# A chain of four attention and feed-forward layers on one core: sums a step sooner, casts in thirds, norms in halves, loads and weight work moved ahead, and an attention with turned keys

## The chip, the cores and the metric

One of the eight cores of a Trainium2 chip runs the whole program in one launch. The metric is the device time of one execution in microseconds (us); smaller is better. The times before are those of three runs; the profile is of one execution more.

## The reference, cut to what matters

x is 16 batches of 56 tokens of 128 features; the context is 16 batches of 1500 rows of 128. Each of four layers adds a cross-attention over the context and then a feed-forward, each on the layer norm of x:

```python
x = x + xattn_i(_layernorm(x), ctx, ...);  x = x + ffn_i(_layernorm(x), ...)   # i = 0, 1, 2, 3
# layers 0 and 3: 16 heads of 8; projections of queries, keys, values, softmax over 1500 keys, output
#   (layer 0 with biases and a mask)
# layer 1: 2 heads of 64; layernorm of the context and once more of x; keys and values are projected
#   from the context and from x (1556 in all); q and k are divided by their rms; masked softmax
# layer 2: 16 heads of 64; layernorm (eps 1e-6) of context, x and output; a null key and value beside
#   the 1500; sim = (xn Wq * scale) (cn Wk)^T; softmax; (attn cn Wv) Wo
# feed-forwards: 0: 8-bit tokens and ternary weights, gelu; 1 and 2: 8 experts, the two best gates
#   (hidden 512 and 256, relu); 3: ternary weights, gelu, layernorm
```

All of it is float32 but the scores of layers 0 and 3, where each factor is split into bfloat16 parts.

## The kernel before, in words

Tokens are held feature-first in xT (128 x 896); a tile is 112 tokens (two batches), 8 tiles in all. `build` runs eight stages in turn: L0a, L0f, L1a, L1f, L2a, L2f, L3a, L3f (attention and feed-forward of each layer). Each stage has a program for each of the five engines (a block), allocates its own tiles and semaphores, and begins with a barrier; `semaphores` clears its semaphores and puts one barrier more at its end. In a stage the order of the work on each engine is written out by hand; engines wait for counts of semaphores. So a stage's first load is issued after the stage before has ended on every engine.

**The norm** (`ln_pe`, `ln_dve`, `ln_pool`, `ln_turn`, lines 97 to 158). TensorE turns the eight token tiles (L100), VectorE takes statistics and adds eps (L133 to L138), GpSimd raises the eight variances to -0.5 (L122), VectorE normalises (L143), TensorE turns the tiles back (L112), VectorE copies (L155, L157). Each step takes all eight tiles before the next begins. In layers 1 and 2, whose attentions take a norm of the norm, the middle part runs twice (eps of two values).

**Attention of small heads** (`attention_16_small_heads`, layers 0 and 3). Eight heads of a batch's 16 make a stack, so there are 32 stacks (two a batch) with four groups of heads each. A step n is one group of one stack, 128 in all, eight a batch (t = n mod 8). In a step TensorE does scores of group n+6 for the maxima (L469 and L477; VectorE reduces them, L780 and L785), turned scores of group n with the maximum subtracted (units S, L504; ScalarE takes the exponential, L647), and the product of probabilities and values of the stack before (L491, part t mod 4 of its chunks). `SmallHeadUnits.of_step` (lines 272 to 290) adds other units to chosen steps: K and V (projections for a later batch, L508, L512), M (the row maxima of a stack, L517, after row_maxima, L792 to L796), R (the sums of the exponentials spread over the rows, L521; VectorE takes the reciprocal and multiplies, L769, L770) and Y (output projection). All units share a ring of four PSUM banks: a unit waits until the fourth before it is emptied, by VectorE (R, Y) or ScalarE (the others). R comes at t=1 and t=5. Stacks' sums are copied by ScalarE (L695) at t=3 and 7, and the values of the next stack wait for that copy. ScalarE also turns the mask to bfloat16 (`float_mask`, L678, t=1, layer 0 only) and the keys to their high bfloat16 part (`key_high`, L689, t=6 in layer 0, t=4 in layer 3), 128 x 1500 each. GpSimd makes the middle and low parts (L596 to L604), and SyncE's queue copies the parts, row by row, to the stacks (L420, L425, L429).

**Attention of layer 1** (`latent_attention`). SyncE loads raw rows and turned rows of a batch two ahead. Per batch: statistics of the raw rows (`stats`, L1218 on), powers on GpSimd, projections K and V, squares and `key_sums`, GpSimd's `key_norm` (L1106, L1110), transposes of the keys (T2), scores, `maximum` (L1268), exponential (L1195), transposes (T3), product (O), transpose (Z), output (Y). Before the loop K and V of batches 0 and 1 are both made, then the first scores.

**Attention of layer 2** (`attention_16_wide_heads`). Wq Wk^T of each head (L1554) and Wv Wo (L1572) are folded to 128 x 128, after VectorE has worked the context norm's scale and bias into Wk and Wv (`weights`, L1742 to L1751). Each batch has 896 rows (16 heads x 56), seven tiles of 128; a step is one tile: three scores matmuls of 501 keys for tile n+2 (L1515), `maximum` on VectorE (L1731), exponential on ScalarE (L1655), 12 transposes of the probabilities in units T0, T1, T2 (L1529), the product with the values in unit O (L1534) of tile n-1, scaled by the reciprocal of the sum by ScalarE (L1646). VectorE normalises the raw rows of the next batch (`normalise`, L1721, t=1 to 3) into V; the keys are V's transposes (unit K, three a batch, L1542, copied by L1707). Unit Z (two a batch, L1546) turns the seven products back. K and Z are `extra(n)` of `WideHeadUnits`. GpSimd raises all variances of the context to -0.5 at the stage's start (L1627) and is idle in the loop. After the loop the output projection runs over all heads (L1608), then a norm and the addition to x.

## Time and profile before

| what | value |
|---|---|
| median of three runs | 2398.16 us (2397.18 to 2400.27) |
| the profiled execution | 2396.25 us, its span 2394.5 us |
| TensorE busy | 2147.7 us (90%), mean granted clock 0.935 |
| VectorE, ScalarE, GpSimd busy | 1443.5, 1203.0, 608.6 us |
| layer 0: attention, feed-forward (TensorE's first and last instruction) | 6 to 455, 456 to 520 |
| layer 1 | 522 to 825, 827 to 946 |
| layer 2 | 949 to 1826, 1830 to 1902 |
| layer 3 | 1905 to 2343, 2344 to 2390 |

```profile
PE   6999999637999698799999999999996889999995
DVE  5677677568888344645544555455434567776775
PEclk8999999757999899799999999999997989999996
```

Each digit is a fortieth of the span, 59.9 us, in tenths of busy time; PEclk is TensorE's granted clock in tenths of 2.4 GHz. The clock falls at the starts of stages, where TensorE is least busy.

### The profile page before, as it was taken

Reading aid. Unit: us, or ns where it says so; the run is one execution under the profiler, and the core shown is the slowest. Engines: PE = TensorE matmul, PEld = TensorE weight load, DVE = VectorE, ACT = ScalarE, POOL = GpSimd, SP = SyncE. Lnnn points to the kernel's source line nnn. Section 1 sums busy time; section 2 is a strip of 40 time slices with the busy share of each in tenths; the row PEclk is TensorE's granted clock in tenths of the full one; section 3 lists DMA queues with packets and bytes.
Section 4 is the critical chain, followed back from the end, with each engine's and each line's share of the span. In section 5 each row is a group of like instructions: output and inputs, shape, how many; then the busy total and the mean of one; then the engine's idle time right before and its main releaser. Section 6 shows DMA issues by size and latency. Waiting matters only on the chain. (4 is left out here: it accounts for less than half of the span.)

```text
span 2394.5 us, 48823 instructions
## 1 busy us (share of the span) xinstructions
PE 2147.7 (90%) x19446; PEld 1583.1 (66%) x19446; DVE 1443.5 (60%) x3160; ACT 1203.0 (50%) x2251; POOL 608.6 (25%) x233
## 2 busy tenths in 40 slices
PE   6999999637999698799999999999996889999995
PEld 3666666426888554467777777777773456766773
DVE  5677677568888344645544555455434567776775
ACT  5777776304666332244444444444430366767761
POOL 7656554004666200600000000000000063433400
PEclk8999999757999899799999999999997989999996
DMA  6444444012442001200000000000000254444420
GB/s 167 139 143 130 137 128 114 14 51 82 132 124 77 19 27 51 59 17 17 20 31 17 17 23 27 17 17 17 1 1 14 64 155 124 122 139 130 115 62 17
DMA packets 87072, 165.19 MB, mean 69 GB/s; under 512 B 40384, under 2 KB 48624, under 8 KB 86592
## 3 DMA queue, kind: packets, MB, share of 16 engines
q1 hardware_dynamic: 86848, 162.08, 23.5%
q8 instruction: 156, 2.56, 0.5%
q14 instruction: 68, 0.56, 0.1%
HBM read 81.75 MB, written 0.46 MB: 34 GB/s over the span
## 5 line engine op out<-in xcount | busy, mean ns | idle before, releaser
L1534 PEld LDWEIGHTS L2ps<-L2values,L2probsT 125*128 125x128 f32 (+1 forms) x2688 | 317.5, 192 | 50.6 <-issue 49.6
L1515 PE MATMUL L2ps<-L2keys,L2qz 128*128 128x501 f32 x672 | 340.1, 590 | 0.9 <-DVE L2out_bias L1778 0.9
L1534 PE MATMUL L2ps<-L2values,L2probsT 125*128 125x128 f32 (+1 forms) x2688 | 318.4, 275 | 0.0
L1731 DVE CUSTOM_DVE_ANT_0 L2work<-L2ps,L2maskadd,L2big 128x1503 f32<-128x1503 f32 x112 | 199.8, 1783 | 163.2 <-PE L2ps L1515 163.2
L122 POOL TENSOR_TENSOR rstd<-mv,half_neg 112x8 f32<-112x8 f32 x9 | 16.8, 1866 | 983.3 <-DVE mv L138 983.3
L1529 PEld LDWEIGHTS L2ps<-const,L2work 128*126 128x126 f32 x1344 | 163.8, 140 | 116.3 <-issue 64.7
L647 ACT ACTIVATE L3probsT<-L3ps 128x448 f32<-128x448 f32 x384 | 191.8, 547 | 84.9 <-PE L3ps L504 84.7
L647 ACT ACTIVATE L0probsT<-L0ps 128x448 f32<-128x448 f32 x384 | 193.0, 550 | 66.1 <-PE L0ps L504 66.0
L1529 PE MATMUL L2ps<-const,L2work 128*126 128x128 f32 x1344 | 202.2, 273 | 1.6 <-ACT L2work L1655 0.9
L785 DVE TENSOR_REDUCE L0partmax<-L0ps 112x1 f32<-112x1000 f32 x128 | 153.3, 1197 | 72.1 <-PE L0ps L477 71.9
L1646 ACT ACTIVATE L2z<-L2ps,L2rinv 128x128 f32<-128x128 f32 x112 | 41.1, 367 | 304.8 <-PE L2ps L1534 304.8
L785 DVE TENSOR_REDUCE L3partmax<-L3ps 112x1 f32<-112x1000 f32 x128 | 153.2, 1197 | 64.1 <-PE L3ps L477 63.8
L1655 ACT ACTIVATE L2work<-L2work,L2negmax 128x1503 f32<-128x1503 f32 x112 | 172.4, 1540 | 15.9 <-DVE L2negmax L1731 15.9
L1639 ACT COPY L2probsT<-L2ps 126x512 f32<-126x512 f32 x224 | 129.5, 578 | 100.3 <-PE L2ps L1529 100.2
L1702 DVE COPY L2probsT<-L2ps 126x512 f32<-126x512 f32 x112 | 77.4, 691 | 147.1 <-PE L2ps L1529 147.1
L504 PEld LDWEIGHTS L3ps<-L3query_stack,L3key_stack 98*128 98x128 bf16 x1536 | 110.6, 99 | 59.2 <-issue 16.3
L504 PEld LDWEIGHTS L0ps<-L0query_stack,L0key_stack 99*128 99x128 bf16 x1536 | 110.4, 99 | 59.6 <-issue 15.5
L504 PE MATMUL L3ps<-L3query_stack,L3key_stack 98*128 98x112 bf16 x1536 | 135.5, 214 | 0.8 <-DVE L3heads_out L770 0.4
L504 PE MATMUL L0ps<-L0query_stack,L0key_stack 99*128 99x112 bf16 x1536 | 135.2, 213 | 0.7 <-ACT L0probsT L647 0.2
L780 DVE TENSOR_REDUCE L0partmax<-L0ps 112x1 f32<-112x500 f32 x128 | 86.4, 675 | 40.0 <-PE L0ps L469 38.3
L780 DVE TENSOR_REDUCE L3partmax<-L3ps 112x1 f32<-112x500 f32 x128 | 86.4, 675 | 38.8 <-PE L3ps L469 37.1
L491 PE MATMUL L0ps<-L0probsT,L0values 128*32 128x112 f32 x3072 | 99.7, 263 | 7.6 <-ACT L0osum L695 7.6
(463 smaller groups left out, 4180.3 us busy)
## 6 DMA issues: line engine op xcount, KB each, us to landing
L0key_stack<-L0key_parts SPq DMA_DIRECT2D x192, 187.5 KB
L3key_stack<-L3key_parts SPq DMA_DIRECT2D x192, 187.5 KB
L0ctxT<-in_ctxT SPq DMA_DIRECT2D x16, 750.0 KB, 4.5
L1raw<-in_ctx SPq DMA_DIRECT2D x16, 750.0 KB
L1rawT<-in_ctxT SPq DMA_DIRECT2D x16, 750.0 KB, 6.2
L2raw<-in_ctx SPq DMA_DIRECT2D x16, 750.0 KB
L3ctxT<-in_ctxT SPq DMA_DIRECT2D x16, 750.0 KB, 4.5
L1fw<-in_L_w SPq DMA_DIRECT2D x16, 256.0 KB, 2.9
```

Of the source, the lines that this page charges most:

```text
L491: last = nc.tensor.matmul(PS[32 * g:32 * g + 32, 3, u * TT:(u + 1) * TT], V[:, b % 2, value_columns(c, 4 * u + g)], PT[:, u, c, g, :], sta ...
L504: last = nc.tensor.matmul(PS[:, bank, c * TT:(c + 1) * TT], KS[:, h % 4, tau, key_columns(4 * j + c)], QS[:, h % 4, tau, :], start=True, s ...
L647: ins = nc.scalar.activation(PT[:, h % 2, 4 * j:4 * j + 4, tau, :], PS[:, bank, 0:HALF].rearrange("p (c n) -> p c n", c=4), ACT.Exp)
L780: nc.vector.tensor_reduce(PM[:, h % 2, tau, 0:1], PS[0:TT, 0, 0:500], AX.X, ALU.max).then_inc(s.m0_done, 1)
L785: nc.vector.tensor_reduce(PM[:, h % 2, tau, 1:2], PS[0:TT, 1:3, 0:500], AX.XY, ALU.max).then_inc(s.m12_done, 1)
L1515: last = nc.tensor.matmul(PS[:, 3 * (m % 2) + c, 0:NPR], tile_rows(m), KT[:, m // RT % 2, 500 * c:500 * c + NPR], start=True, stop=True)
L1529: last = nc.tensor.transpose(PS[0:CH + 1, bank, c * P:(c + 1) * P], PR[:, i % 2, at:at + CH + 1], k.ident)
L1534: last = nc.tensor.matmul(PS[:, bank, 0:P], PT[0:keys_in(c), i % 2, c, :], V[0:keys_in(c), i // RT % 2, c, :], start=c == 0, stop=c == NCH ...
L1639: ins = nc.scalar.copy(PT[:, i % 2, 4 * j:4 * j + 4, :].rearrange("p c n -> p (c n)"), PS[0:CH + 1, bank, :])
L1655: nc.scalar.activation(PR[:, m % 2, :], SM[:, m % 2, :], ACT.Exp, bias=nmax[:, m % 4:m % 4 + 1], scale=-1.0, accum_out=ssum[:, m % 4:m % 4 ...
L1702: ins = nc.vector.tensor_copy(PT[:, i % 2, 4 * j:4 * j + 4, :].rearrange("p c n -> p (c n)"), PS[0:CH + 1, bank, :])
L1731: nc.vector.tensor_tensor_reduce(SM[:, m % 2, :].rearrange("p (c n) -> p c n", c=3), PS[:, 3 * (m % 2):3 * (m % 2) + 3, 0:NPR], MA[:, m // ...
```

## The change

The norm works in halves of four tiles, and the norm of a norm becomes one pass: its variance v gives v (1 + eps2) + eps1 eps2, and one power is taken.

```diff
+    for h in range(2):
+        pe.wait_ge(s.ln_norm, h + 1)
+        for t in range(4):
+            last = nc.tensor.transpose(ps[:, 2 + h, t * TT:(t + 1) * TT], k.xn[:, 4 * h + t, :], k.ident[0:TT, 0:TT])
+        last.then_inc(s.ln_feat, 1)
...
+def ln_pool(pool, k, s):
     nc = k.nc
-    for n in range(len(eps)):
-        pool.wait_ge(s.ln_var, n + 1)
-        nc.gpsimd.tensor_tensor(k.rstd[:], k.mv[:, :, 1], k.half_neg[0:TT, 0:NTT],
+    for h in range(2):
+        pool.wait_ge(s.ln_var, h + 1)
+        nc.gpsimd.tensor_tensor(k.rstd[:, 4 * h:4 * h + 4], k.mv[:, 4 * h:4 * h + 4, 1], k.half_neg[0:TT, 0:4],
                                 ALU.pow).then_inc(s.ln_rstd, 1)
...
+    for h in range(2):
+        tiles = range(4 * h, 4 * h + 4)
+        dve.wait_ge(s.ln_tok, h + 1)
+        for t in tiles:
             last = nc.vector.bn_stats(k.stats[:, t, :], src(t))
         link(last)
...
+        var = k.mv[:, 4 * h:4 * h + 4, 1]
+        if len(eps) == 1:
+            last = nc.vector.tensor_scalar(var, var, eps[0], None, ALU.add)
+        else:
+            last = nc.vector.tensor_scalar(var, var, 1.0 + eps[1], eps[0] * eps[1], ALU.mult, ALU.add)
+        last.then_inc(s.ln_var, 1)
...
+    for h in range(2):
+        dve.wait_ge(s.ln_rstd, h + 1)
+        for t in range(4 * h, 4 * h + 4):
...
-    last.then_inc(s.ln_norm, 1)
+        last.then_inc(s.ln_norm, 1)
```

In the small heads R moves to t=0 and t=4, and the two casts are made in thirds of 500 columns, at t=0, 1, 2 (mask) and t=6, 7, 8 (high part in layer 0) or 3, 4, 5 (layer 3).

```diff
-        if t == 1 and 0 <= 2 * b - 2 < HB:
+        if t == 0 and 0 <= 2 * b - 2 < HB:
             own.append(("R", 2 * b - 2, 0, "D"))
-        if t == 5 and 0 <= 2 * b - 1 < HB:
+        if t == 4 and 0 <= 2 * b - 1 < HB:
             own.append(("R", 2 * b - 1, 0, "D"))
...
-                nc.scalar.copy(KP[:, b % 2, 0], KF[:, b % 2, :]).then_inc(s.hi_ready, 1)
+            def float_mask(b, thirds=range(3)):
+                for j in thirds:
+                    if j == 0:
+                        wait_mask(act, b)
+                        if b:
+                            act.wait_ge(s.keys_masked, b)
+                    at = slice(j * 500, (j + 1) * 500)
+                    nc.scalar.copy(MF[:, at], MR[:, b % 2, at]).then_inc(s.mask_float, 1)
...
+            def key_high(b, thirds=range(3)):
+
+                for j in thirds:
+                    if masked:
+                        act.wait_ge(s.keys_masked, b + 1)
+                    else:
+                        wait_emptied(act, plan.emptied("K", b, j))
+                    if b >= 2 and j == 0:
+                        wait_stacked(act, 2 * b - 4)
+                        wait_stacked(act, 2 * b - 3)
+                    at = slice(j * 500, (j + 1) * 500)
+                    nc.scalar.copy(KP[:, b % 2, 0, at], KF[:, b % 2, at]).then_inc(s.hi_ready, 1)
...
-                if masked and n % 8 == 1 and 3 <= n // 8 + 3 < B:
-                    float_mask(n // 8 + 3)
-                if n % 8 == (6 if masked else 4) and 3 <= n // 8 + 3 < B:
-                    key_high(n // 8 + 3)
+                if masked and n % 8 in (0, 1, 2) and 3 <= n // 8 + 3 < B:
+                    float_mask(n // 8 + 3, [n % 8])
+                b, j = divmod(n - (6 if masked else 3), 8)
+                if j < 3 and 3 <= b + 3 < B:
+                    key_high(b + 3, [j])
```

`LatentAhead` owns the tiles of layer 1's loads, and its seven first loads are issued in the feed-forward of layer 0 (`ahead.sync(sp)`, behind that stage's own). In layer 1 batch 1's K and V, its squares and its statistics are placed behind the first scores.

```diff
+    def sync(self, sp):
+        sp.dma_start(self.W[:], self.src["L1_attn_w"]).then_inc(self.s.w_loaded, 16)
+        for b in range(2):
+            self.load_raw(sp, b)
+            self.load_turned(sp, b)
+            self.load_mask(sp, b)
...
-    units = kv(0, (0, 1)) + kv(0, (2,)) + kv(1, (0, 1)) + kv(1, (2,)) + turned_keys(0)
+    units = kv(0, (0, 1, 2)) + turned_keys(0) + kv(1, (0, 1, 2))
...
-            for what, j in (("K", 0), ("V", 0), ("K", 1), ("V", 1)):
-                unit(what, 0, j)
...
-            unit("K", 0, 2)
-            unit("V", 0, 2)
+            for j in range(3):
+                unit("K", 0, j)
+                unit("V", 0, j)
...
-            for what, j in (("K", 0), ("V", 0), ("K", 1), ("V", 1)):
-                unit(what, 1, j)
...
-            unit("K", 1, 2)
-            unit("V", 1, 2)
             for j in range(3):
                 unit("T2", 0, j)
             scores(0, range(4))
+            for j in range(3):
+                unit("K", 1, j)
+                unit("V", 1, j)
...
+            stats(0)
+            dve.wait_ge(s.qk_filled, 1)
...
-            last.then_inc(s.vl_ready, 1)
+            key_sums(0)
+            stats(1)
...
-            empty("K", 1, 2)
             empty("T2", 0, 1)
+            maximum(0)
+            for j in range(3):
+                empty("K", 1, j)
             stats(2)
             key_sums(1)
```

`WideAhead` does the same for layer 2's weights in layer 1's feed-forward: loads, the work of `weights` on GpSimd, with the sums on VectorE before the experts 5 and 6 (`vector`), and the powers of the context's variances.

```diff
+    def sync(self, sp):
+        s = self.s
+        for n in (1, 2, 0, 3):
+            sp.dma_start(self.W[:, n], self.src["L2_attn_w"][:, n]).then_inc(s.w_loaded, 16)
...
+        pool.wait_ge(s.w_loaded, 64)
...
+        for n in (1, 2):
+            w = self.W[:, n]
+            nc.gpsimd.tensor_tensor(self.products[:, n - 1], w, self.ROWS[:, 1:2, :].to_broadcast([64, 16, P]), ALU.mult
+                                    ).then_inc(s.products, 1)
+            pool.wait_ge(s.products, n)
+            nc.gpsimd.tensor_tensor(w, w, self.ROWS[:, 0:1, :].to_broadcast([64, 16, P]), ALU.mult).then_inc(s.scaled, 1)
+            pool.wait_ge(s.scaled, n)
+            nc.gpsimd.tensor_tensor(w[:, :, 0:P - 1], w[:, :, 0:P - 1], w[:, :, P - 1:P].to_broadcast([64, 16, P - 1]),
+                                    ALU.subtract).then_inc(s.centred, 1)
+        pool.wait_ge(s.ve_ready, 1)
+        for pair in range(B // 2):
+            at = self.rs[:, 2 * pair:2 * pair + 2, :].rearrange("p b c -> p (b c)")
+            nc.gpsimd.tensor_tensor(at, at, self.k.half_neg[0:CH, 0:24], ALU.pow).then_inc(s.spread, 1)
...
+    def vector(self, dve, link, n):
+
+        nc, s = self.nc, self.s
+        dve.wait_ge(s.products, n)
+        link(nc.vector.tensor_reduce(self.U[:, n - 1], self.products[:, n - 1], AX.X, ALU.add))
+        dve.wait_ge(s.centred, n)
+        dve.wait_ge(s.rows_loaded, 48)
+        nc.vector.tensor_scalar(self.W[:, n, :, P - 1], self.U[:, n - 1], -1.0, self.NKV[:, n - 1:n], ALU.mult, ALU.add
+                                ).then_inc(s.summed, 1)
```

In layer 2 the units K (but for batch 0) and Z are gone. The turned rows of the context are loaded into the key tile, and GpSimd subtracts the mean and multiplies by the reciprocal deviation; both are written once to DRAM and loaded per batch, spread over 127 partitions. O's operands are exchanged, so that its product comes out turned, and the division by the sum is made on the probabilities before their transposes (`scale`, on VectorE).

```diff
+        SCALE_OF = WQK[:].rearrange("p h n -> p (h n)")[0:P - 1, 0:S2]
...
+            def load_keys(b):
+                if b == 1:
+                    sp.wait_ge(s.slot_ready, 2)
+                    sp.wait_ge(s.q_filled, 2 * H)
+                else:
+                    sp.wait_ge(s.scores_filled, RT * (b - 1))
+                    sp.wait_ge(s.keys_scaled, b - 1)
+                sp.dma_start(KT[0:P - 1, b % 2, 0:S2], src["ctxT"][b][0:P - 1]).then_inc(s.key_parts, 16)
+                for x, to in enumerate((MEAN[0:P - 1], SCALE_OF)):
+                    sp.dma_start(to, scratch[x, b].rearrange("c n -> (c n)").partition_broadcast(P - 1)).then_inc(s.key_parts, 16)
...
+            sp.wait_ge(s.moments_ready, 1)
+            sp.dma_start(scratch.rearrange("k (h b) c n -> (b c) (k h) n", h=2), MOMENTS[:]).then_inc(s.moments_stored, 16)
+            sp.wait_ge(s.moments_stored, 16)
+            load_keys(1)
...
+                    if m == 0:
                         for j in range(3):
-                            wait_emptied(pe, plan.emptied("K", m // RT, j))
+                            wait_emptied(pe, plan.emptied("K", 0, j))
+                    elif m % RT == 0:
+                        pe.wait_ge(s.keys_scaled, m // RT)
...
-                        pe.wait_ge(s.exp_done, i + 1)
+                        pe.wait_ge(s.scaled, i + 1)
...
-                        last = nc.tensor.matmul(PS[:, bank, 0:P], PT[0:keys_in(c), i % 2, c, :], V[0:keys_in(c), i // RT % 2, c, :],
+                        last = nc.tensor.matmul(PS[:, bank, 0:P], V[0:keys_in(c), i // RT % 2, c, :], PT[0:keys_in(c), i % 2, c, :],
...
-                elif what == "Z":
-                    wait_emptied(pe, plan.emptied("O", RT * i + (6 if j else 3), 0))
-                    for t in range(3 if j else 4):
-                        last = nc.tensor.transpose(PS[:, bank, t * P:(t + 1) * P], ZB[:, j, t, :], k.ident)
...
+            for n in range(4):
+                half_of = slice(n % 2 * (B // 2), n % 2 * (B // 2) + B // 2)
+                of = rs[:, half_of, :] if n >= 2 else k.ctx_mv[:, half_of, :, 0]
+                last = nc.tensor.transpose(PS[0:B // 2 * NCH, 5, n * CH:(n + 1) * CH], of.rearrange("p b c -> p (b c)"),
+                                           k.ident[0:CH, 0:CH])
...
-            for pair in range(B // 2):
...
+            nc.gpsimd.memset(KT[:, 1, :], 0.0).then_inc(s.slot_ready, 1)
+            pool.wait_ge(s.slot_ready, 1)
+            nc.gpsimd.tensor_copy(KT[:, 1, S2:S2 + 1], k.ident[:, P - 1:P]).then_inc(s.slot_ready, 1)
+            for b in range(1, B):
+                pool.wait_ge(s.key_parts, 48 * b)
+                nc.gpsimd.tensor_tensor(KT[0:P - 1, b % 2, 0:S2], KT[0:P - 1, b % 2, 0:S2], MEAN[0:P - 1], ALU.subtract
+                                        ).then_inc(s.keys_moved, 1)
+                pool.wait_ge(s.keys_moved, b)
+                nc.gpsimd.tensor_tensor(KT[0:P - 1, b % 2, 0:S2], KT[0:P - 1, b % 2, 0:S2], SCALE_OF, ALU.mult
+                                        ).then_inc(s.keys_scaled, 1)
...
-                    g = t // 4
-                    if b:
-                        act.wait_ge(s.filled, plan.filled("Z", b - 1, g))
-                    act.wait_ge(s.rinv_ready, i + 1)
-                    ins = nc.scalar.mul(ZB[:, g, t % 4, :], PS[:, bank, 0:P], rinv[:, i % 4:i % 4 + 1])
+                    ins = nc.scalar.copy(tile_rows(i), PS[:, bank, 0:P])
...
-                    if i >= 2:
-                        dve.wait_ge(s.scores_filled, RT * (i - 1))
                     ins = nc.vector.tensor_copy(KT[:, i % 2, 500 * j:500 * j + n], PS[:, bank, 0:n])
-                elif what == "Z":
-                    n = (3 if j else 4) * P
-                    ins = nc.vector.tensor_copy(QZ[:, i, 4 * P * j:4 * P * j + n], PS[:, bank, 0:n])
...
+            def scale(m):
+
+                dve.wait_ge(s.exp_done, m + 1)
+                nc.vector.reciprocal(rinv[:, m % 4:m % 4 + 1], ssum[:, m % 4:m % 4 + 1]).then_inc(s.rinv_ready, 1)
+                dve.wait_ge(s.rinv_ready, m + 1)
+                nc.vector.tensor_scalar(PR[:, m % 2, :], PR[:, m % 2, :], rinv[:, m % 4:m % 4 + 1], None, ALU.mult
+                                        ).then_inc(s.scaled, 1)
...
+            scale(0)
             for n in range(plan.last_step + 1):
                 b, t = divmod(n, RT)
                 if plan.first(n):
                     empty(*plan.first(n))
-                if n < RT * B:
-                    dve.wait_ge(s.exp_done, n + 1)
-                    if n >= 4:
-                        dve.wait_ge(s.emptied_a, plan.emptied("O", n - 4, 0)[1])
-                    nc.vector.reciprocal(rinv[:, n % 4:n % 4 + 1], ssum[:, n % 4:n % 4 + 1]).then_inc(s.rinv_ready, 1)
-                if plan.extra(n):
-                    empty(*plan.extra(n))
                 if t in (1, 2, 3) and b + 1 < B:
                     normalise(b + 1, t - 1)
+                if n + 1 < RT * B:
+                    scale(n + 1)
                 if n + 2 < RT * B:
                     maximum(n + 2)
```

## Rows read from the trace of the kernel before

**Rows 1.** Stretches: each engine's busy time (instructions), granted clock, DMA share, GB/s.

```profile
60.00:440.00 380.00, 360.10 (x5379) 261.34 (x5381) 268.78 (x458) 276.22 (x541) 192.78 (x67) 1.00 0.44 125
...
522.00:586.00 64.00, 38.14 (x223) 33.19 (x223) 47.41 (x181) 15.73 (x32) 24.94 (x12) 0.66 0.33 103
...
949.00:1023.00 74.00, 51.42 (x191) 33.40 (x192) 44.00 (x95) 14.82 (x25) 41.51 (x14) 0.71 0.29 69
...
1040.00:1790.00 750.00, 748.61 (x4932) 587.05 (x4930) 372.03 (x688) 346.07 (x565) 0.00 (x0) 1.00 0.06 18
```

**Rows 2.** Timeline, layer 0: start, us, engine, line, operation, tiles, [idle <-releaser].

```profile
234.10 0.38 PE L469 MATMUL L0ps<-L0key_stack,L0query_stack 97*112 97x500 bf16 x1
...
235.67 0.85 DVE L769 RECIPROCAL L0ps<-L0ps 128x112 f32<-128x112 f32 x1
...
236.88 0.36 PE L517 MATMUL L0ps<-L0ident_bf,L0maxparts 112*3 112x112 bf16 x4 [0.74 <-DVE L0heads_out L770]
...
238.31 0.38 PE L469 MATMUL L0ps<-L0key_stack,L0query_stack 97*112 97x500 bf16 x1
...
248.43 0.38 PE L469 MATMUL L0ps<-L0key_stack,L0query_stack 97*112 97x500 bf16 x1
...
252.10 0.38 PE L469 MATMUL L0ps<-L0key_stack,L0query_stack 97*112 97x500 bf16 x1
...
254.18 0.38 PE L469 MATMUL L0ps<-L0key_stack,L0query_stack 97*112 97x500 bf16 x1
...
255.34 0.78 PE L491 MATMUL L0ps<-L0probsT,L0values 128*32 128x112 f32 x24 [0.59 <-ACT L0osum L695]
...
257.81 0.38 PE L469 MATMUL L0ps<-L0key_stack,L0query_stack 97*112 97x500 bf16 x1
```

**Rows 3.** Timeline, layer 3: the same wait.

```profile
2103.06 0.36 PE L517 MATMUL L3ps<-L3ident_bf,L3maxparts 112*2 112x112 bf16 x4 [0.74 <-DVE L3heads_out L770]
```

**Rows 4.** Timeline, layer 2's loop: a step with K, one with neither.

```profile
1286.09 0.60 PE L1529 MATMUL L2ps<-const,L2work 128*126 128x128 f32 x4
...
1287.81 0.59 PE L1542 MATMUL L2ps<-const,L2values 125*128 125x125 f32 x4
1288.24 1.01 PE L1515 MATMUL L2ps<-L2keys,L2qz 128*128 128x501 f32 x2
...
1293.04 0.60 PE L1529 MATMUL L2ps<-const,L2work 128*126 128x128 f32 x4
...
1306.95 0.60 PE L1529 MATMUL L2ps<-const,L2work 128*126 128x128 f32 x4
...
1307.42 1.54 ACT L1655 ACTIVATE L2work<-L2work,L2negmax 128x1503 f32<-128x1503 f32 x1
...
1310.99 1.78 DVE L1731 CUSTOM_DVE_ANT_0 L2work<-L2ps,L2maskadd,L2big 128x1503 f32<-128x1503 f32 x1 [2.64 <-PE L2ps L1515]
...
1313.47 0.60 PE L1529 MATMUL L2ps<-const,L2work 128*126 128x128 f32 x4
```

**Rows 5.** Layer 1's and 3's starts, and a group (busy, mean ns | idle).

```profile
552.49 0.69 DVE L1291 TENSOR_SCALAR L1keysT<-xnT,vec 128x896 f32<-128x896 f32 x1
...
1905.39 1.32 DVE L801 TENSOR_SCALAR L3head_scale<-const 128x2 f32<-128x2 f32 x1 [1.14 <-PEq L78]
...
L598 POOL TENSOR_TENSOR L3keys<-L3keys,L3key_parts 128x1500 f32<-128x1500 f32 x16 | 48.6, 3035 | 200.5 <-ACT L3key_parts L689 200.5
```

**Rows 6.** Timeline, layer 1's start (the stage begins at 522.1).

```profile
534.22 2.42 DVE L1218 BATCH_NORM_STATS2 L1st<-L1raw 125x6 f32<-125x128 f32 x12 [6.97 <-DMA L1raw<-in_ctx]
...
586.13 1.78 DVE L1268 CUSTOM_DVE_ANT_0 L1masked<-L1ps,L1maskadd 112x1556 f32<-112x1556 f32 x1 [1.16 <-PE L1ps L1031]
```

**Rows 7.** Timeline, layer 2's start (the stage begins at 949.0).

```profile
980.54 20.93 PE L1566 MATMUL L2ps<-xnT,L2wqk 128*128 128x448 f32 x46 [1.49 <-DVE xnT L157]
...
1020.73 8.25 PE L1515 MATMUL L2ps<-L2keys,L2qz 128*128 128x501 f32 x12 [0.87 <-DVE L2out_bias L1778]
```

**Rows 8.** Timeline, layer 1's feed-forward, its norm.

```profile
832.64 2.64 DVE L143 TENSOR_SCALAR xn<-L1fps,mv,rstd 112x128 f32<-112x128 f32 x8 [1.76 <-POOL rstd L122]
...
837.13 1.16 DVE L155 COPY xnT<-L1fps 128x448 f32<-128x448 f32 x2 [1.85 <-PE L1fps L112]
```

357 lines of the change are left out of this document (159 added, 198 removed).

## The prediction

> **What bounds it now.** I read the stretches first [rows 1]: in the small-head loop of layer 0 TensorE is busy 360 of 380 us, in the wide-head loop of layer 2 748.6 of 750. There the time is TensorE's own list plus its stalls. In the two stretches between loops (522 to 586, 949 to 1023) it is busy only 38 and 51 us, at a granted clock of 0.66 and 0.71; there the longest chain through VectorE, GpSimd and the loads counts. Then the timelines. A step of the small-head loop is the distance between two L469 matmuls. The eight steps of a batch repeat to 0.01 us in twelve batches: 4.21, 2.98, 3.87, 3.26, 3.67, 2.08, 3.63, 2.35, sum 26.05; [rows 2] show four of them. The step without additions lasts 2.08 (252.10 to 254.18). In layer 2 a batch is 47.70: steps of 6.95 where a unit K or Z is added, 6.52 where none is [rows 4], all gapless. The change is therefore priced per step in the loops and along a chain in the prologues.
>
> **Small heads, sums sooner.** M (L517) starts at 236.88 after 0.74 idle, released by L770, which follows the reciprocal at 235.67, which stands behind row_maxima in VectorE's order [rows 2]. Without the stall the step of 4.21 is 2.08 + 0.28 (M) + 0.90 (K, 2.98 - 2.08) = 3.26: the stall is 0.95. The step of 3.67 has 2.08 + 0.28 + 0.89 (V): 0.41. The edit puts R a step earlier, in steps without row_maxima, so M waits for ScalarE units only. What is late next is row_maxima itself: R (1.13 us) in t=0 moves max0 of t=1 back to 2.03 after the step's start, so the maxima are ready 2.08 into t=2, where M wants to start at 1.9: 0.25 stays. In t=4 R is emptied 4.26 into a step of 4.14, and the first S of t=5 waits for it at 4.35: no stall, with 0.1 to spare. Gain 0.70 x 15 + 0.41 x 14 = 16.2. Layer 3 stalls the same way [rows 3]: 16.1 more. Bounds: 6 if the tight place in t=4 opens, 20 if no remainder stays.
>
> **Casts in thirds.** In layer 0 the whole cast on ScalarE delays the copy of the sums, and the values matmul waits 0.59 at 255.34; the step of 3.63 should be 2.97 (Y costs 0.89) [rows 2]. Three casts of about 0.6 for one of 1.45 add 0.7 us to a ScalarE that then has 21.4 of about 24.5 us filled; by adding up the steps it falls 0.8 us behind in t=6 to 2 (mask third and key third meet in t=0), and the copy of the sums comes 0.2 late. I take 0.45 x 12 = 5.4. Bounds: 7.9 and -6 (two units of the ring late per batch). The parts of the keys get ready 4 us later; their slot comes free only about then, and the stack lands 8 us before its first scores. The first stack is on the chain: +0.7. Layer 3's ScalarE has no mask to cast: 0. Layer 0 in all: -20.8 (with its share of 16.1).
>
> **Layer 2's loop.** Transposes K: 12 a batch, 0.43 for 4 (1287.81 to the next S) [rows 4]; Z: 7 a batch, 0.43 and 0.33. 3 x 0.43 + 0.76 = 2.05 a batch, and all steps become 6.52: 15 x 2.05 = 30.8, and 1.9 in the last batch with its emptying. The exchanged operands of O keep count and sizes: 0 (bounds +-0.02 a step). New on VectorE: scale(n+1), 1503 columns in place. A like instruction took 0.69 for 896 columns [rows 5], so about 1.0; bound above 1.6 (no faster than a cycle an element). Its place: exp ends 2.3 after the first transpose of a step (1307.42 + 1.7 - 1306.95), scale runs from 2.5 to 3.7, the maximum waits for its scores till 4.04 (1310.99) and ends at 5.9, exp needs it at 7.0 [rows 4]. With normalise (1.05 us) before it, scale ends at 4.0; both hide. TensorE waits for scale(n+1) only at the next step. Cover gone by over a microsecond, each microsecond more costs 112.
>
> GpSimd, idle until now in this loop, gets two operations of 3.04 a batch [rows 5]. Two numbers there say that the two engines keep each other out: L801, two elements wide, took 1.32, as long as GpSimd's memset that ran beside it. A scale held up by 3.0 pushes the exponential back by about 1.3 at worst. One scale in each batch can be met: 0 to 20 in all; I take 4. The Trainium skill ("SBUF — State Buffer", section "SBUF: two separate sides") says that the shared port pair is an exclusive lock, held for a whole instruction, for a VectorE instruction in a two-port mode against GpSimd. The trace agrees (the 1.32 us). The mechanism's own price, if both operations of a batch reached TensorE at full length, is rival (e).
>
> Keys: three loads of 762 KB a batch, 2.3 MB, then 6.1 us of GpSimd, from two steps before a batch to two steps before the next, 45.6 us. At the 69 GB/s that [rows 1] show at worst, 33 + 6.1: hidden. Loop: 32.7 - 4 = -28.7.
>
> **Layer 2's start.** Old: first scores 71.7 us after the stage's start (949.0 to 1020.73), projection of the queries from 980.54 [rows 7]. The weight work moves into layer 1's feed-forward: GpSimd there six operations of some 4.1 and eight of 4.5 (61 us; from the weights' landing near 845 it ends before 920, the stage at 946); VectorE two sums of 2.3 that fit its waits of 2.8 for TensorE. New chain: tokens 1.0, norm 5.9, folds meanwhile on TensorE to 9.5, turning and copies to 12.2, then 32 projections. Before, these ran 1.5 us each for the first 5 us and 0.75 after; I keep that (clock at 1.2 GHz after the sparse matmuls before them): 27.4 with normalise(0). Then 3.8 each for the folds of the values, the bias and the first keys: 51.0. Gain 20.7; less 2.3, since scale(0) stands behind maximum(1). -18.4; bounds -27 (2.4 GHz throughout) and -6 (1.2 GHz as long as before).
>
> **Layer 1's start.** VectorE waited 6.97 us for the raw rows, and the first maximum came 64 us in [rows 6]. All six loads now lie in layer 0's feed-forward, whose queue is empty; its own weights go first. One pass of the norm less is 4.8 us. Along the new order: norm 7.4, folds and turning 11.5, stats(0) 15.1, query copies and K(0) 20.4, squares and sums 27.6, powers and norm on GpSimd 35.6, queries turned 38.6, scores 45.2: the first maximum 18.7 sooner. But K and V of batch 1, stats(2) and key_sums(1) now come behind it, and GpSimd's norm of batch 1 ends at 64: the second maximum at 72 where it was at 83.3. -11.3; bounds -4 and -19.
>
> **Norms in halves.** The power on GpSimd (1.76 idle) and the turning (1.85 idle, then both copies) are overlapped with the other half [rows 8]: 1.5 net of the added instructions, 1.5 for the turning, 0.5 to 0.9 for tokens. Layer 0's feed-forward 1.5 (no turning; VectorE starts there with the weights' sums), layer 1's 3.3, layer 2's output 3.3, its feed-forward 3.7, layer 3's 3.0 (waits for weights). In layers 0 and 3 attention the keys' chain is longer: 0. Less 1.0, where GpSimd's weight work meets the gates: -13.8; bounds -8 and -16. Two more groups of semaphores to clear: +0.6 (1.38 between layer 2's stages, which clears two, against 1.15).
>
> **Sum** against the profiled execution, 2396.25 (span 2394.5; median of the runs 2398.16, 0.08% above): 20.8 + 16.1 + 28.7 + 18.4 + 11.3 + 13.8 - 0.6 = 108.5, so 2288.
>
> **Rivals.** (a) Prologues and thirds give little: the waits are handed to the next late chain (GpSimd's powers in layer 1, the 1.2 GHz clock in layer 2), the thirds cost as much as they give. What is left are the steps TensorE doesn't have to run: 16 + 14 + 27 + 6 + 4 + 8, less 5: about 2326. For it: TensorE had work from 970, and the projections from 980.54 still ran at 1.5 us each for 5 us. (b) TensorE stays at 2.4 GHz through both prologues, and nothing meets on the port: 2396 less 128 = 2268. Against it: both stretches still hold gaps of several microseconds. (c) Slower: the keys come late. One row sent to 127 partitions is no load that these rows show at this size. With everything else as forecast (80 us), the kernel gets slower once the chain of loads and two operations takes over 47.7 + 80 / 15 = 53 us; at 60 us it gives 2316 + 15 x 12.3 = 2500. Against it: 33 us at the worst rate. (d) The change doesn't do what it says in the small heads: S of t=5 waits for R as long as M did before, 2288 + 32 = 2320. For it: 0.1 us of margin. (e) GpSimd's two operations hold VectorE off for their whole 6.1 us, and TensorE waits: 2288 - 4 + 15 x 6.1 = 2375. For it: L801 [rows 5]; against it: a hold-up of 3.0 meets 1.7 us of slack between scale, maximum and exponential.
>
> **Chances.** Forecast 0.60, (a) 0.17, (b) 0.09, (c) 0.05, (d) 0.05, (e) 0.04. A change under 0.2% can't be told from none here; only a (c) of just 53 us gives that: 0.01 of its 0.05, so faster 0.95, slower 0.04; I shade this to 0.93, 0.02 and 0.05 for what six edits at once may do to each other. The range goes from (b) to just beyond (a): 2265 to 2332.
>
> **What would show it.** Layer 2: all steps 6.52, exp_done to scale short, GpSimd's key operations done long before the batch; wrong, if L1529's first transpose waits for the scaling. Small heads: batches of 24.0 to 24.6, no idle before L517 from L770; wrong, if S of t=5 waits for R. Layer 1: no load wait at the first statistics, first maximum near 45. Layer 2's first scores near 51. The forecast fails by more than its range only if a batch of layer 2 isn't about 45.6.

## The result: slower by 28%, because the keys of layer 2 come late

The changed kernel takes 3067.59 us (median; 3061.77 to 3077.04), the kernel before 2397.67. The ratio is 1.2796, interval 1.2761 to 1.2831. Forecast were 2288 and a range of 2265 to 2332: wrong in sign and size. What happened is rival (c), to which the prediction gave 0.05.

The page of the changed kernel, its 40 slices (76.7 us each):

```profile
PE   7999975899698456533664336643466388899996
POOL 6556602566340000000000000000000000544320
PEclk8999985999798778766887678866787688999997
GB/s 151 154 147 139 129 83 22 125 115 58 49 35 38 35 37 26 36 36 36 37 26 36 36 36 28 34 36 36 37 26 35 14 8 58 142 141 135 130 109 14
```

TensorE is half idle from the 14th to the 32nd slice, and the core moves mostly 26 to 38 GB/s there, against 130 to 150 in layers 0 and 3. The costliest group says who is waited for, and the stretch says how much (columns as in [rows 1] and [rows 5]):

```profile
L1596 PE MATMUL L2ps<-L2keys,L2qz 128*128 128x501 f32 x672 | 366.9, 631 | 731.5 <-POOL L2keys L1713 730.6
L1710 POOL TENSOR_TENSOR L2keys<-L2keys,L2mean_spread 127x1500 f32<-127x1500 f32 x15 | 50.1, 3339 | 1388.1 <-DMA L2wqk<-L_moments 1388.1
...
1040.00:2480.00 1440.00, 727.29 (x4456) 551.49 (x4457) 422.83 (x694) 326.95 (x544) 100.17 (x30) 0.75 0.09 32
```

The 730.6 us are 15 waits, one a batch: six steps of a batch last 6.52 us, the seventh (t=5, in which the first scores of the next batch stand) 54.1 to 59.4. Who makes GpSimd wait stands in the DMA queue of SyncE; a long row there is an issue that SyncE could not finish:

```profile
1260.91 0.23 SPq L1569 DMA_DIRECT2D L2keys<-in_ctxT  x1
1261.18 0.54 SPq L1571 DMA_DIRECT2D L2mean_spread<-L_moments  x1
1261.77 29.86 SPq L1571 DMA_DIRECT2D L2wqk<-L_moments  x1
1291.67 28.93 SPq L1552 DMA_DIRECT2D L2raw<-in_ctx  x1
1320.64 17.14 SPq L1557 DMA_DIRECT2D L2mask<-in_mask_full  x1
...
1350.56 3.34 POOL L1710 TENSOR_TENSOR L2keys<-L2keys,L2mean_spread 127x1500 f32<-127x1500 f32 x1 [89.72 <-DMA L2wqk<-L_moments]
1353.98 3.34 POOL L1713 TENSOR_TENSOR L2keys<-L2keys,L2wqk 127x1500 f32<-127x1500 f32 x1
...
1357.46 2.01 PE L1596 MATMUL L2ps<-L2keys,L2qz 128*128 128x501 f32 x2 [48.45 <-POOL L2keys L1713]
```

From the issue at 1260.91 to the landing at 1350.5 pass 89.6 us for three loads of 127 rows, 29.9 each. With GpSimd's 6.8 that makes 96.4, and the next loads are issued at 1357.39: loads and operations form one ring, because mean and deviation have one tile each. While only these loads run, packets of 6000 bytes end every 0.229 us, one after the other:

```profile
1265.00:1290.00 25.00, 25.00 (x163) 19.42 (x162) 14.18 (x22) 10.20 (x18) 0.00 (x0) 0.99 0.07 27
```

A DMA share of 0.07 is one sixteenth: one of the core's 16 DMA engines works. 127 packets x 0.229 = 29.1 us. After each idle stretch TensorE starts again at 1.2 GHz (granted clock 0.50 from 1357.4 to 1359.5; the first two scores above took 2.01 us, 1.01 in the running loop). The loop's excess over steps of 6.52 is 767 us, 730.6 of it waiting; the other 2.4 us a batch go with these slow restarts.

By stage, TensorE's first to last instruction, in us, one profiled execution of each kernel. The last column is the changed kernel with two repairs (below), in which nothing hides the other steps:

| stage | before | forecast change | changed kernel | with both repairs |
|---|---|---|---|---|
| layer 0 attention | 448.6 | -20.8 | 430.1 (-18.5) | 427.7 (-20.9) |
| its feed-forward | 63.2 | -1.5 | 62.0 (-1.2) | 62.0 (-1.2) |
| layer 1 attention | 303.4 | -11.3 | 292.3 (-11.1) | 291.8 (-11.6) |
| its feed-forward | 118.9 | -2.3 | 129.5 (+10.6) | 117.3 (-1.6) |
| layer 2 attention | 876.8 | -50.4 | 1588.6 (+711.8) | 816.9 (-59.9) |
| its feed-forward | 72.7 | -3.7 | 69.1 (-3.6) | 69.0 (-3.7) |
| layer 3 attention | 437.2 | -16.1 | 425.1 (-12.1) | 422.4 (-14.8) |
| its feed-forward | 45.8 | -3.0 | 42.9 (-2.9) | 43.0 (-2.8) |

Six of eight stages lie within 4 us of the forecast; layer 2's attention is off by 762. The second, small miss is layer 1's feed-forward, by 13. Its gates' chain on VectorE (rows of the timeline; GpSimd's operations below):

```profile
814.22 0.20 DVE L2251 CAST L1fgate_short<-L1fgate 112x64 bf16<-112x64 f32 x1
814.45 0.20 DVE L2252 CAST L1fgate_parts<-L1fgate_short 112x64 f32<-112x64 bf16 x1
814.56 4.52 DVE L2253 TENSOR_TENSOR L1fgate<-L1fgate,L1fgate_short 112x64 f32<-112x64 f32 x1
819.12 4.50 DVE L2254 CAST L1fgate_short<-L1fgate 112x64 bf16<-112x64 f32 x1
823.65 3.61 DVE L2255 CAST L1fgate_parts<-L1fgate_short 112x64 f32<-112x64 bf16 x1
827.18 0.21 DVE L2256 TENSOR_TENSOR L1fgate_parts<-L1fgate,L1fgate_short 112x64 f32<-112x64 f32 x1
...
814.50 4.50 POOL L1421 TENSOR_TENSOR L2qz<-L2work,L2lnc_rows 64x2048 f32<-64x2048 f32 x1 [13.17 <-DMA L2nkv<-in_L_null]
819.08 4.49 POOL L1424 TENSOR_TENSOR L2work<-L2work,L2lnc_rows 64x2048 f32<-64x2048 f32 x1
823.64 3.57 POOL L1426 TENSOR_TENSOR L2work<-L2work 64x2032 f32<-64x2032 f32 x1
```

Three instructions of 0.2 us last exactly as long as the GpSimd operation beside each. 12.0 us are lost, and TensorE waits 11.8 us for the gates' parts.

### The profile page after: what moved, and what is told of

Its sections match the earlier page's. It is cut to its first block and busy times, and to the rows that moved or that the text cites. A ratio compares the mean times of both kernels' runs of the same rounds, so it can differ in the third digit from the quotient of the medians.

```text
span 3067.4 us, 48086 instructions
## 1 busy us (share of the span) xinstructions
PE 2150.3 (70%) x19158; PEld 1575.0 (51%) x19158; DVE 1501.3 (49%) x3143; ACT 1208.0 (39%) x2353; POOL 730.9 (24%) x278
## 3 DMA queue, kind: packets, MB, share of 16 engines
q1 hardware_dynamic: 93008, 196.56, 20.9%
## 5 line engine op out<-in xcount | busy, mean ns | idle before, releaser
L1596 PE MATMUL L2ps<-L2keys,L2qz 128*128 128x501 f32 x672 | 366.9, 631 | 731.5 <-POOL L2keys L1713 730.6
L1596 PEld LDWEIGHTS L2ps<-L2keys,L2qz 128*128 128x128 f32 x672 | 110.8, 207 | 738.3 <-issue 737.1
L1710 POOL TENSOR_TENSOR L2keys<-L2keys,L2mean_spread 127x1500 f32<-127x1500 f32 x15 | 50.1, 3339 | 1388.1 <-DMA L2wqk<-L_moments 1388.1
L1615 PEld LDWEIGHTS L2ps<-L2probsT,L2values 125*128 125x128 f32 (+1 forms) x2688 | 317.5, 192 | 51.5 <-issue 49.9
L1615 PE MATMUL L2ps<-L2probsT,L2values 125*128 125x128 f32 (+1 forms) x2688 | 318.4, 275 | 0.5 <-ACT L2probsT L1725 0.5
L1610 PEld LDWEIGHTS L2ps<-const,L2work 128*126 128x126 f32 x1344 | 173.0, 146 | 135.0 <-issue 133.1
L1610 PE MATMUL L2ps<-const,L2work 128*126 128x128 f32 x1344 | 212.2, 282 | 3.5 <-DVE L2work L1817 3.1
L1727 ACT COPY L2qz<-L2ps 128x128 f32<-128x128 f32 x112 | 29.7, 265 | 305.7 <-PE L2ps L1615 305.7
L1817 DVE TENSOR_SCALAR L2work<-L2work,L2rinv 128x1503 f32<-128x1503 f32 x112 | 112.3, 1003 | 3.9
L791 DVE TENSOR_REDUCE L0partmax<-L0ps 112x1 f32<-112x500 f32 x128 | 86.2, 673 | 33.6 <-PE L0ps L474 33.5
```

Of the source, the lines that this page charges most:

```text
L791: nc.vector.tensor_reduce(PM[:, h % 2, tau, 0:1], PS[0:TT, 0, 0:500], AX.X, ALU.max).then_inc(s.m0_done, 1)
L1596: last = nc.tensor.matmul(PS[:, 3 * (m % 2) + c, 0:NPR], tile_rows(m), KT[:, m // RT % 2, 500 * c:500 * c + NPR], start=True, stop=True)
L1610: last = nc.tensor.transpose(PS[0:CH + 1, bank, c * P:(c + 1) * P], PR[:, i % 2, at:at + CH + 1], k.ident)
L1615: last = nc.tensor.matmul(PS[:, bank, 0:P], V[0:keys_in(c), i // RT % 2, c, :], PT[0:keys_in(c), i % 2, c, :], start=c == 0, stop=c == NCH ...
L1817: nc.vector.tensor_scalar(PR[:, m % 2, :], PR[:, m % 2, :], rinv[:, m % 4:m % 4 + 1], None, ALU.mult).then_inc(s.scaled, 1)
```

## Experiments

All stand beside runs of the kernel before on the same chip, but not all on one chip: the kernel before took 2397.3 us beside e1, e3, e4 and e5, 2399.3 beside e6 to e9 and 2402.0 (one run) beside e2 and e10. Between these groups a distance of medians is good to a few us only; there the ratios and the stages of the traces count. Stages whose code an edit leaves alone differ by up to 4 us between the profiled executions: in the nine kernels that have the changed kernel's code there, layer 0's attention took 427.7 to 431.2 us and layer 3's 422.4 to 426.3, most of it at the start of the loops.

First, what makes a load of 127 rows slow.

**e1_112**

```diff
-    sp.dma_start(KT[0:P - 1, b % 2, 0:S2], src["ctxT"][b][0:P - 1]).then_inc(s.key_parts, 16)
-    for x, to in enumerate((MEAN[0:P - 1], SCALE_OF)):
-        sp.dma_start(to, scratch[x, b].rearrange("c n -> (c n)").partition_broadcast(P - 1)).then_inc(s.key_parts, 16)
+    for lo, hi in ((0, 112), (112, 127)):
+        sp.dma_start(KT[lo:hi, b % 2, 0:S2], src["ctxT"][b][lo:hi]).then_inc(s.key_parts, 16)
+    for lo, hi in ((0, 112), (112, 127)):
+        for x, to in enumerate((MEAN[lo:hi], SCALE_OF[lo:hi])):
+            sp.dma_start(to, scratch[x, b].rearrange("c n -> (c n)").partition_broadcast(hi - lo)).then_inc(s.key_parts, 16)
```

> The changed kernel with one edit: each of the three key loads of a batch in layer 2 is cut into two DMAs, rows 0 to 111 and rows 112 to 126. Theory A (a load of 127 rows runs on one DMA engine, one 6000-byte packet each 0.229 us, so 29.1 us a load): 112 rows are 7 packets on each of 16 engines, 1.6 us, the loads leave the path, all batches of layer 2's loop last 45.6 us as the fourth steps now wait for nothing, and the time is 3067.6 less the waits above 6.52 us in the loop (767 us): 2300 us. Theory B (sending one row of DRAM to many partitions is slow by itself): two loads of three stay at 29 us, a batch takes 67 us, 2620. Theory C (GpSimd's two key operations, now beside a running loop, hold VectorE up for their whole length): 2300 + 15 x 6.7 = 2400.

Measured 2303.04, ratio 0.9611 (0.9594 to 0.9628). Theory A: the bytes are the same, and the loss is gone. A batch lasts 45.64 us throughout, but for one of 45.91. GpSimd's first operation starts 13.4 us after the issue instead of 89.6. Right behind the issues of a batch (1156.46 to 1159.1) all 16 DMA engines work (the last three numbers are the clock, the DMA share and GB/s):

```profile
1158.00:1164.00 6.00, 6.00 (x39) 4.52 (x39) 3.04 (x6) 2.89 (x5) 0.00 (x0) 1.00 1.00 292
```

Theory C falls too: the operations meet VectorE now, and the steps stay. Of 112 scales 18 overlap an operation and 14 are held by it. The timeline at the worst of them:

```profile
1259.17 4.17 DVE L1819 TENSOR_SCALAR L2work<-L2work,L2rinv 128x1503 f32<-128x1503 f32 x1
1259.19 3.35 POOL L1712 TENSOR_TENSOR L2keys<-L2keys,L2mean_spread 127x1500 f32<-127x1500 f32 x1 [36.88 <-DMA L2wqk<-L_moments]
...
1263.26 1.77 DVE L1810 CUSTOM_DVE_ANT_0 L2work<-L2ps,L2maskadd,L2big 128x1503 f32<-128x1503 f32 x1
```

The scale takes 4.17 us for 1.00; the step it is in takes 6.79 for 6.52. All the rest is slack.

**e2_keys** cuts only the load of the turned rows; its diff to e1_112 is

```diff
     for lo, hi in ((0, 112), (112, 127)):
         sp.dma_start(KT[lo:hi, b % 2, 0:S2], src["ctxT"][b][lo:hi]).then_inc(s.key_parts, 16)
-    for lo, hi in ((0, 112), (112, 127)):
+    for lo, hi in ((0, 127),):
         for x, to in enumerate((MEAN[lo:hi], SCALE_OF[lo:hi])):
```

and **e3_spreads**, the other way round, has `((0, 127),)` in the first of these loops and cuts only the two spreading loads.

> The changed kernel with only the load of the turned rows cut at row 112; the two spreading loads stay whole (127 rows). Theory A (every load of 127 rows takes 29.1 us on one engine, and the loads of a batch, GpSimd's 6.8 us and the next batch's loads form one chain): 58.2 + 3 + 2.2 + 6.8 = 70 us at most, 68 at least, for a batch, so 2303 + 15 x 23.5 = 2655. Theory B (the loads of a batch would run side by side on other engines if the first did not block them): 2303.

> The changed kernel with only the two loads that spread mean and deviation cut at row 112; the load of the turned rows stays whole (127 rows). Theory A (one engine for 127 rows): the chain of a batch is 29.1 + some 3 + 2.2 us until all has landed + 6.8 of GpSimd = 41 us, under the 45.6 of the loop, so the time is that of e1_112, 2300. Theory B (a load of 29 us also holds back the raw rows and the mask on the same queue): waits of a few us at every fourth step, 2300 to 2400.

Measured 2654.55 and 2309.29 (one run each, profiled). Each load left whole costs its 29 us of the ring, until the ring is shorter than the batch: the operations start every 70.1 to 71.1 us with two whole loads (72.5 the first time). That e2_keys meets the expected 2655 to the microsecond is in part luck: layer 2's attention is 366 us longer than in e1_112, not 352, and layer 1's feed-forward, which the edit leaves alone, is 16 us shorter (see e5_gates). With one whole load the ring is about as long as the batch, 45 to 47 us, longer than the 41 expected, since the last spreading load is issued only some 18 us behind the whole one; a step is late by up to 1.3 us in nine batches, and the first batch loses 3.8. So e3 lies 6 us above e1_112 (9 us in layer 2's attention), as its theory B has it in part: a slow load holds back what is issued behind it. The spreading as such is cheap. GpSimd's first operation in e2_keys:

```profile
1226.34 3.34 POOL L1712 TENSOR_TENSOR L2keys<-L2keys,L2mean_spread 127x1500 f32<-127x1500 f32 x1 [63.62 <-DMA L2wqk<-L_moments]
1296.56 3.34 POOL L1712 TENSOR_TENSOR L2keys<-L2keys,L2mean_spread 127x1500 f32<-127x1500 f32 x1 [63.45 <-DMA L2wqk<-L_moments]
```

**e4_113**: all three cut at row 113, a prime.

```diff
-    for lo, hi in ((0, 112), (112, 127)):
+    for lo, hi in ((0, 113), (113, 127)):
```

> The changed kernel with the three key loads cut at row 113 instead of 112 (rows 0 to 112, and 14 rows). Theory A (the number of engines is the largest number up to 16 that divides the rows; 113 is a prime): each big load still runs on one engine, 113 x 0.229 = 25.9 us, a batch takes 97 - 3 x 3.2 = 87 us, and the time is 2300 + 15 x 42 = 2930. Theory B (only the full length of 127 rows is badly placed, or the size of a DMA counts): like e1_112, 2300.

Measured 2930.19 (one run), where A said 2930; again the exact number is partly luck. The operations start every 88 to 90 us, not 87, and layer 2's attention is 639 us longer than in e1_112, while layer 1's feed-forward is 15 us shorter there. So one row more in the large part costs 639 us in its stage, and issues behind such a load stand for 25.4 to 26.1 us, with a DMA share of 0.07:

```profile
1228.46 25.51 SPq L1573 DMA_DIRECT2D L2wqk<-L_moments  x1
```

Neither the length nor the size of a DMA decides, but whether the number of rows can be divided over the engines.

**e10_gpsimd**: the whole loads of 127 rows again, issued by GpSimd (this one and all that follow have the repair of the gates, next).

```diff
+    pool.dma_start(KT[0:P - 1, b % 2, 0:S2], src["ctxT"][b][0:P - 1]).then_inc(s.key_parts, 16)
+    for x, to in enumerate((MEAN[0:P - 1], SCALE_OF)):
+        pool.dma_start(to, scratch[x, b].rearrange("c n -> (c n)").partition_broadcast(P - 1)).then_inc(s.key_parts, 16)
     pool.wait_ge(s.key_parts, 48 * b)
```

> The changed kernel with the gates' order of e5_gates, all three key loads whole (127 rows), but issued by GpSimd on its own queue, right before it waits for them. Theory A (the split over engines follows the same division of rows whoever issues): 29.1 us a load as before, 3067.6 less 21 = 3046. Theory B (GpSimd's queue spreads 127 rows over 16 engines, as the Trainium skill, DMA: Bandwidth & Descriptors, section Why a DMA increments its semaphore by 16 and not by 1, states for some direct copies): the chain of a batch is 3 x 2 + some 5 us for issuing and landing + 6.8 = 18 us, hidden, time 2282 to 2290. Theory C (the keys were late because the raw rows and the mask lay ahead of them on SyncE's queue): one engine, but no queueing, 87 + 6.8 = 94 us a batch, 3010.

Measured 2288.8 (one run), its theory B. In the timeline the three loads of 127 rows are issued in 1.6 us, and GpSimd's first operation starts 12.7 us after the first issue:

```profile
1233.09 0.57 POOL L1704 DMA_DIRECT2D L2keys<-in_ctxT  x1 [26.18 <-PE L2ps L1584]
1233.65 0.52 POOL L1706 DMA_DIRECT2D L2mean_spread<-L_moments  x1
1234.16 0.52 POOL L1706 DMA_DIRECT2D L2wqk<-L_moments  x1
1245.76 3.36 POOL L1708 TENSOR_TENSOR L2keys<-L2keys,L2mean_spread 127x1500 f32<-127x1500 f32 x1 [11.07 <-DMA L2wqk<-L_moments]
```

```profile
1235.00:1245.00 10.00, 10.00 (x64) 7.51 (x63) 5.24 (x8) 5.26 (x9) 0.00 (x0) 1.00 0.96 221
```

2.29 MB in 12.7 us are 180 GB/s where one engine gave 27, and the DMA share meanwhile is 0.96: all 16 engines. So of the two queues tried only SyncE's puts 127 rows on one engine. The Trainium skill ("DMA: Bandwidth & Descriptors", section "Why a DMA increments its semaphore by 16 and not by 1") states both: a DMA runs on the largest number of engines up to 16 that divides the slowest dimension (here the rows) of both its sides, with 127 as an example for one engine, and, as an exception on trn2, GpSimd's queue gives some direct copies all 16. The runs agree: 29 us behind each load of 127 rows and 26 behind one of 113 on SyncE's queue, and 12.7 us for three loads of 127 from GpSimd.

**e5_gates**: e1_112, and GpSimd waits for the gates' parts before the weight work.

```diff
             if ahead:
+                pool.wait_ge(s.parts_ready, 1)
                 ahead.gpsimd(pool)
```

> As e1_112, and in layer 1's feed-forward GpSimd begins layer 2's weight work only after VectorE has made the parts of the gates. Theory A (a copy on VectorE that meets a GpSimd operation waits for its end: three copies of 64 elements took 4.5, 4.5 and 3.6 us in the changed kernel): the gate chain loses some 11.5 us, the stage goes from 129.5 to 118, and the time is 11.5 below e1_112, about 2288.5. Theory B (the gates are late because the weights' loads share the queue or the memory): within 1 us of e1_112.

Measured 2282.01, ratio 0.9521 (0.9505 to 0.9537), the fastest kernel here, 4.8% under the one before. It is 21.0 below e1_112, not 11.5. Theory A is right and its size was taken from another run: in e1_112 four gate instructions were held, not three, and the stage took 133.2 us, now 117.3: 15.9. All of the chain now take 0.19 to 0.22:

```profile
811.74 0.22 DVE L2256 TENSOR_TENSOR L1fgate<-L1fgate,L1fgate_short 112x64 f32<-112x64 f32 x1
811.99 0.19 DVE L2257 CAST L1fgate_short<-L1fgate 112x64 bf16<-112x64 f32 x1
812.22 0.20 DVE L2258 CAST L1fgate_parts<-L1fgate_short 112x64 f32<-112x64 bf16 x1
```

The repair makes certain what is otherwise a matter of one microsecond. Without it the weight work starts when the weights have landed: 17.7 to 18.0 us after the stage's start in the changed kernel, e1_112 and e3_spreads, in the middle of the gates' chain, which ends at 18.9 to 19.3 if nothing holds it. In e2_keys and e4_113 they landed later, the work started at 18.8 and 19.8, no gate was held, and the stage took 117.2 and 118.2 us with no repair. In e2_keys:

```profile
812.60 0.22 DVE L2258 TENSOR_TENSOR L1fgate_parts<-L1fgate,L1fgate_short 112x64 f32<-112x64 f32 x1
812.72 4.52 POOL L1421 TENSOR_TENSOR L2qz<-L2work,L2lnc_rows 64x2048 f32<-64x2048 f32 x1 [13.94 <-DMA L2nkv<-in_L_null]
```

The rest came in layer 2's start: the granted clock of its first 10 us is 0.84 here and 0.55 in e1_112, the projections begin 2.7 us sooner, and the first scores start at 45.2 after the stage's start, not 49.2. The eleven kernels with the new start fall into two groups. Where gates were held (the changed kernel, e1_112, e3_spreads) TensorE runs at 1.2 GHz for 13.6 us and the first scores start at 48.9 to 49.2; in the eight others for 3.4 us and at 45.1 to 45.2. In its last 20 us before the stage TensorE runs the same 56 matmuls in both. Why the clock goes with the gates isn't shown.

Then the parts of the forecast that the late keys had covered, each undone in e5_gates. These four ran on another chip than e5_gates, so the distances by stage come from the traces.

**e6_sums**

```diff
-        if t == 0 and 0 <= 2 * b - 2 < HB:
+        if t == 1 and 0 <= 2 * b - 2 < HB:
             own.append(("R", 2 * b - 2, 0, "D"))
-        if t == 4 and 0 <= 2 * b - 1 < HB:
+        if t == 5 and 0 <= 2 * b - 1 < HB:
```

> e5_gates with the unit R back at t=1 and t=5 (casts still in thirds). Theory A (R before row_maxima in VectorE's order is what M waited for): in both small-head layers the step t=2 goes from 3.50 back to 4.21 and t=6 from 3.46 to 3.67, the other steps sum to the same, a batch is 25.40 instead of 24.48 (0.92 more, 15 batches in each layer), and the time is 27 us above e5_gates (2282.0), 2309. Theory B (the thirds alone freed ScalarE, and M would not wait any more wherever R stands): within 4 us of e5_gates.

Measured 2311.46, ratio 0.9633 (0.9618 to 0.9647): 29 us above e5_gates by the medians, 27 by the ratios, theory A. In the traces layer 0's attention is 17.4 us longer and layer 3's 15.0. A batch in the middle of the loop is 25.38 to 25.41 in both layers (but for one of layer 0 near its start, 29.4, the cause of which wasn't looked for, some 4 us), and the wait is back with its old length [rows 2]:

```profile
339.86 0.36 PE L522 MATMUL L0ps<-L0ident_bf,L0maxparts 112*3 112x112 bf16 x4 [0.74 <-DVE L0heads_out L781]
```

In the changed kernel the same matmul has no wait, and the step is 3.50 (252.92 to 256.42):

```profile
252.92 0.38 PE L474 MATMUL L0ps<-L0key_stack,L0query_stack 97*112 97x500 bf16 x1
...
255.00 0.36 PE L522 MATMUL L0ps<-L0ident_bf,L0maxparts 112*3 112x112 bf16 x4
...
256.42 0.38 PE L474 MATMUL L0ps<-L0key_stack,L0query_stack 97*112 97x500 bf16 x1
```

**e7_whole**

```diff
-                if masked and n % 8 in (0, 1, 2) and 3 <= n // 8 + 3 < B:
-                    float_mask(n // 8 + 3, [n % 8])
+                if masked and n % 8 == 1 and 3 <= n // 8 + 3 < B:
+                    float_mask(n // 8 + 3)
...
-                    nc.scalar.copy(MF[:, at], MR[:, b % 2, at]).then_inc(s.mask_float, 1)
+                nc.scalar.copy(MF[:], MR[:, b % 2, :]).then_inc(s.mask_float, 3)
```

> e5_gates with the two casts of the small heads made whole again (R stays at t=0 and t=4). Theory A (thirds give only the wait for the copy of the sums in layer 0, 1.57 - 0.90 = 0.67 a batch, the difference of what a batch gained in layer 0 and in layer 3): layer 0's batch 25.15, layer 3's 24.48, the first stack 0.7 sooner, time 7 us above e5_gates, 2289. Theory B (the thirds cost as much as they give, ScalarE being late in the steps around them): within 2 us of e5_gates.

Measured 2288.99, ratio 0.9539 (0.9523 to 0.9555), 7 above e5_gates by the medians, 4 by the ratios: the intervals overlap, but the steps are plain. The keys' cast is made whole in the same way. Layer 0's batch is 25.15 and layer 3's 24.48, as A has it; the values matmul waits 0.58 us for the copy of the sums again, and layer 0's attention is 6.8 us longer. The thirds have a price in the loop's first batch: it takes 23.9 us with whole casts (24.1 in the kernel before) and 25.9 to 28.8 in the ten kernels with thirds, least in e5_gates. So their net gain in layer 0's attention is 3 to 7 us. Why that batch gets longer isn't shown.

**e8_loads**

```diff
 def bitlinear_ffn(nc, k, src, ahead=None):
...
-            if ahead:
-                ahead.sync(sp)
...
 def latent_attention(nc, k, src, ahead):
...
+            ahead.sync(sp)
             for b in range(2, 4):
```

> e5_gates with layer 1's seven first loads issued at the start of layer 1 again instead of in layer 0's feed-forward; the new order of the work in layer 1 stays. Theory A (the order and the norm's one pass gave the gain; the raw rows land 12.1 us after the stage's start, as before, and stats(0) now begins at 10.8): the first maximum at 44 to 45 us instead of 42.7, time 1 to 2 us above e5_gates, 2283.5. Theory B (the wait of 7.0 us for the raw rows was what the loads ahead removed): 7 us above, 2289.

Measured 2288.22, ratio 0.9536 (0.9521 to 0.9552); inconclusive in the time (the four runs lie at 2284.6, 2285.1, 2291.4 and 2291.7), so the trace has to tell. In it layer 1's attention is 2.9 us longer than in e5_gates; 7.3 us more lie in the attentions of layers 0 and 3, which this edit leaves alone. The first maximum starts 46.5 us after the stage's start (42.7 in e5_gates, 64.0 before [rows 6]). The statistics start 2.1 later, at 12.9. The other 1.7 are the scores, the same eight matmuls, which take 4.44 us here and 2.75 in e5_gates (second row), after a longer idle stretch:

```profile
545.13 4.44 PE L1050 MATMUL L1ps<-L1keysT,L1queries 128*112 128x389 f32 x8 [1.95 <-DVE L1keysT L1268]
```

```profile
539.54 2.75 PE L1049 MATMUL L1ps<-L1keysT,L1queries 128*112 128x389 f32 x8 [0.76 <-DVE L1keysT L1267]
```

The clock was 0.62 there and 1.00 in e5_gates. So of the 21.3 us by which the first maximum came sooner the loads ahead gave some 2 to 4, and the order and the single pass of the norm, not told apart here, 17.5.

**e9_double**

```diff
-    nc.gpsimd.tensor_tensor(KT[0:P - 1, b % 2, 0:S2], KT[0:P - 1, b % 2, 0:S2], MEAN[0:P - 1], ALU.subtract
+    for i, op in enumerate((ALU.subtract, ALU.add, ALU.subtract)):
+        nc.gpsimd.tensor_tensor(KT[0:P - 1, b % 2, 0:S2], KT[0:P - 1, b % 2, 0:S2], MEAN[0:P - 1], op
```

> e5_gates with four GpSimd operations on the keys of each batch in layer 2 instead of two (the mean subtracted, added back, subtracted again). Theory A (an operation holds up a scale on VectorE until it ends, so by up to 3.2 us, seen in 18 of 112 in e1_112, and the slack between scale, maximum and exponential takes that up): some 32 scales are long, nearly all steps stay at 6.52, and the time is 0 to 4 us above e5_gates, 2284. Theory B (operations back to back hold VectorE over their whole length): 15 x 6.7 = 100 us above, 2382.

Measured 2295.0, ratio 0.9562 (0.9547 to 0.9576), 13 above e5_gates by the medians, 10 by the ratios: neither theory's number. In the trace 3.4 us lie in layer 3, which this edit doesn't touch, 3.3 in layer 2's start; 8.1 are in layer 2's loop, mostly at its step t=1, in nearly every batch (up to 7.8 us), the fourth operation reaching the steps in which the values are normalised:

```profile
1065.64 3.53 DVE L1820 TENSOR_SCALAR L2work<-L2work,L2rinv 128x1503 f32<-128x1503 f32 x1
1069.10 1.77 DVE L1811 CUSTOM_DVE_ANT_0 L2work<-L2ps,L2maskadd,L2big 128x1503 f32<-128x1503 f32 x1
...
1071.40 5.04 DVE L1801 TENSOR_SCALAR L2values<-L2raw,ctx_mv,L2rs 125x127 f32<-125x127 f32 x4
```

A hold-up of 2.5 us is absorbed once; a second one in the next step (four of 0.34 take 5.04) is not.

## Why the prediction was wrong, and where it was right

**The step that failed** is the sentence on the keys: "At the 69 GB/s that [rows 1] show at worst, 33 + 6.1: hidden." The three loads take 89.6 us, not 33. The 69 GB/s were the mean of a stretch with many transfers in it, not the rate of one transfer, and they were no bound. No row of the kernel before shows a load of 127 rows; the cost was unknown and had to be bounded by what one DMA engine gives. The trace of the kernel before held a hint: its raw rows are loaded with 125 rows of 6144 bytes (L1482), issued at 1290.16, and a little later the DMA share is 0.32, about five sixteenths, at 130 GB/s:

```profile
1294.00:1297.00 3.00, 3.00 (x18) 1.98 (x17) 1.12 (x3) 1.94 (x4) 0.00 (x0) 1.00 0.32 130
```

Five is the largest number up to 16 that divides 125, and five times the 27 GB/s of one engine are, as an estimate, 135; by the same count 127, a prime, leaves one engine. The prediction even named the place ("no load that these rows show at this size") and gave it 0.05. Rival (c)'s own formula with the measured ring, 2316 + 15 x (97.0 - 47.7) = 3056, comes within 12 us of 3067.6. Its mechanism, "sent to 127 partitions", was half right: e2_keys and e3_spreads show that the plain load of 127 rows costs the same 29 us as a spread one, and e4_113 that it is the number of rows. GpSimd's two operations, 6.1 us in the forecast, took 6.8.

**Layer 2's loop otherwise**: all steps 6.52 in e5_gates, 45.64 a batch as forecast, O's exchange 0. The 4 us for GpSimd and VectorE keeping each other out were 0 to 0.3: the scale was held up, by 0.3 to 3.2 us, in 14 of 112 cases, as the rival (e) has it, but the slack of scale, maximum and exponential took it.

**Layer 2's start**: first scores at 48.9 (forecast 51.0) in the changed kernel. The 2.3 for scale(0) were 2.8 (2.2 in e5_gates), counted from the first scores to the transposes of the third tile. The projections lasted 27.0 (forecast 27.4), with the slow clock at their start as assumed; e5_gates' 25.1 is what a faster clock is worth.

**Gates**: the 1.0 for "where GpSimd's weight work meets the gates" was 12.0, and 15.9 in e1_112. The rule had been read from L801 [rows 5] and applied to layer 2's loop, where slack absorbs it, but not to the chain of small operations where nothing does. There it acts per instruction: each of 0.2 us waits for a whole one of 3.6 to 4.5.

**Small heads**: M at t=2 stalls 0.25 (3.50 for 3.26, as forecast); at t=6 0.20 stays where 0 was forecast (3.46), which is 3 of the missing us in each layer; in t=4 R costs no stall (4.10). A batch is 24.48, in the range named. e6_sums gives the edit 27 to 29 us in all, forecast 32.3. The thirds give 0.67 a batch, 8 in 12 batches, less 2 to 5 in the first batch; forecast 5.4 less 0.7.

**Layer 1's start**: first maximum at 42.9 (forecast 45), second at 72.1 (forecast 72), stage -11.1 (forecast -11.3). The norms are within 0.4 us of the forecast in every feed-forward but layer 1's.

So the sum of the terms without the keys was sound: 2288 forecast, 2282 with both repairs. Layer 2's attention gave 59.9 instead of 50.4: the 4 us for the two engines keeping each other out fell away, and the first scores came 5.8 us before the forecast, 3.7 of it by the faster clock. The forecast had kept the slow clock of the kernel before, so this part was not foreseen.

## What to carry to other kernels

Before a load goes on a critical ring, look at how its rows divide: on SyncE's queue here three loads of 112 + 15 rows were in use 13.4 us after their issue, three of 127 after 89.6. Never bound one transfer by the GB/s of a busy stretch; a row with the same number of rows and the same issuing engine is needed, and without one the lower bound is one DMA engine. And GpSimd work "in the background" costs most where VectorE runs a chain of short instructions, each of which can wait for a whole GpSimd operation; whether they meet can hang on one microsecond of a load's landing, so order them with a semaphore.

## What the runs showed of the hardware that was not expected

- One DMA engine moves a 6000-byte packet in 0.229 us, 26 GB/s (the stretch's row says 27), and the number of engines of a SyncE load hangs on its rows: 127 or 113 rows gave a DMA share of 0.07, 125 rows 0.32, 112 rows, with other loads beside them, 1.00. GpSimd's queue had no such limit at 127 rows (0.96).
- A SyncE issue behind such loads stands still for 29 us (L1552 above), so loads that are themselves well divided come late too.
- VectorE's copy from SBUF to SBUF, its scale, its normalisation and a two-operand operation were held by GpSimd; the maximum (L1810) and the copies that read PSUM kept their 1.78 and 0.69 us beside it in e1_112 and e5_gates.
